# A Mamba block with a routed feed-forward: GpSimd's inflows of four units moved behind the scatters of their unit, and the scatters and lists laid out anew

## What is computed

```python
x = x + attn_ref(layernorm(x))        # attn_ref: below
x = x + ffn_ref(layernorm(x))         # top 2 of 8 experts, gated, width 344

# inside attn_ref, for each token l, channel d (256) and state n (16)
delta = softplus(dt @ dt_w.T + dt_b)
dA = exp(delta * A)                   # "decay"
dBu = delta * B * xc                  # "inflow"
h = dA * h + dBu                      # along the tokens: "scan", "state"
y = sum over n of h * C               # "product", summed on TensorE
y = (y + xc * D) * silu(z)            # then out_proj, and the feed-forward
```

## Time and profile before

| | |
|---|---|
| median of 3 runs | 848.82 us (848.8 to 850.25) |
| the profiled execution, its own time | 843.71 us |
| its span, first to last instruction | 841.0 us |
| VectorE busy | 739.6 us, 88% |
| TensorE busy (matmuls) | 649.6 us, 77% |
| GpSimd busy | 580.0 us, 69% |
| ScalarE busy | 506.9 us, 60% |
| mean granted clock of TensorE | 0.89 |

### The profile page before, as it was taken

The page is one execution under the profiler, slowest core; times in us unless marked ns, Lnnn a source line. Parts: engine busy times, 40 slices in busy tenths (PEclk is TensorE's granted clock), DMA queues, the critical chain, the costliest instruction groups (busy, mean ns, idle before and its releaser), DMA issues.

```text
span 841.0 us, 12622 instructions
## 1 busy us (share of the span) xinstructions
PE 649.6 (77%) x3545; PEld 465.1 (55%) x3545; DVE 739.6 (88%) x1147; ACT 506.9 (60%) x1091; POOL 580.0 (69%) x487
## 2 busy tenths in 40 slices
PE   4438688878778877787967877986876889898992
PEld 2124455545355536764657635863554556788992
DVE  1376998989999999999999999999999898686676
ACT  2545895876678577565856567464864775444441
POOL 1095675677977797688958897689855995456542
PEclk9659898989989898997889989897877899999996
DMA  6933233222323335543364336532423520123139
GB/s 177 269 97 101 91 111 111 83 88 90 115 75 101 104 105 182 160 134 114 114 192 135 107 101 189 154 124 97 132 86 104 179 85 24 45 55 93 54 102 272
DMA packets 80295, 99.92 MB, mean 119 GB/s; under 512 B 10263, under 2 KB 48099, under 8 KB 80211
## 3 DMA queue, kind: packets, MB, share of 16 engines
q1 hardware_dynamic: 75907, 90.21, 35.9%
q0 software_dynamic: 4320, 8.92, 3.0%
HBM read 87.56 MB, written 15.35 MB: 122 GB/s over the span
## 4 chain that ended last, share of the span: by engine, by line
DVE 36%; PE 33%; issue 18%; ACT 6%; POOL 4%; DMA 2%; SPq 1%; DVEq 1%; ACTq 0%; POOLq 0%
DVE state L1092 18%; PE work_front L1270 4%; DVE product L1102 4%; PE y L1310 4%; PE up L1432 2%; PE up L1421 2%; PE work_front L1276 2%; PE y L1306 2%; PE gate L1414 2%; POOL inflow L833 2%; DVE stats L1022 2%; ACT decay L956 1%; DVE silu_m L1235 1%; DVE arena L1067 1%; PE work_side L1354 1%
## 5 line engine op out<-in xcount | busy, mean ns | idle before, releaser
L833 POOL TENSOR_TENSOR inflow<-du,b_wide 128x1024 f32<-128x1024 f32 x128 | 315.5, 2468 | 145.1 <-DVE product L1102 92.1
L1092 DVE TENSOR_TENSOR_SCAN state<-decay,carry,inflow 128x512 f32<-128x512 f32 x192 | 234.8, 1264 | 6.5 <-ACT decay L956 6.5
L1102 DVE TENSOR_TENSOR product<-state,c_wide 128x1024 f32<-128x1024 f32 (+1 forms) x93 | 138.9, 1494 | 4.4 <-PE y L1306 3.3
L956 ACT ACTIVATE decay<-arena,a_neg 128x512 f32<-128x512 f32 x128 | 86.6, 688 | 60.6 <-DVE state L1092 56.8
L1306 PE MATMUL y<-ident,product 128*128 128x128 f32 x664 | 106.5, 305 | 20.5 <-DVE product L1102 20.5
L1306 PEld LDWEIGHTS y<-ident,product 128*128 128x128 f32 x664 | 87.4, 158 | 62.5 <-issue 34.7
L956 ACT ACTIVATE decay<-delta_odd,a_neg 128x512 f32<-128x512 f32 x128 | 86.5, 688 | 56.2 <-DVE state L1092 56.0
L863 POOL DMA_INDIRECT y_dram<-y_rows,x_rows x71 | 81.6, 1149 | 55.9 <-ACT y_rows L1012 49.2
L1310 PE MATMUL y<-h_rows,ident 128*128 128x512 f32 x180 | 100.9, 652 | 7.1 <-ACT h_rows L921 6.5
L857 POOL DMA_INDIRECT row_dram<-m_tok,place x64 | 74.2, 1159 | 24.4 <-issue 12.9
L1092 DVE TENSOR_TENSOR_SCAN state<-decay,inflow 128x512 f32<-128x512 f32 x64 | 74.5, 1203 | 6.1 <-ACT decay L956 3.6
(11 more groups left out here) (232 smaller groups left out, 1342.5 us busy)
## 6 DMA issues: line engine op xcount, KB each, us to landing
b_wide<-bc_dram SPq DMA_DIRECT2D x128, 256.0 KB, 3.3
c_wide<-bc_dram SPq DMA_DIRECT2D x93, 256.0 KB, 3.5
w_stage<-gate_up_dram SPq DMA_DIRECT2D x26, 344.0 KB, 4.4
x_rows<-row_dram SPq DMA_DIRECT2D x71, 65.0 KB, 2.1
arena<-gate_up_dram SPq DMA_DIRECT2D x8, 344.0 KB, 4.2
x_tok<-in_x SPq DMA_DIRECT2D x8, 256.0 KB, 5.8
out<-x_tok SPq DMA_DIRECT2D x7, 256.0 KB, 4.9
inflow<-y_dram SPq DMA_DIRECT2D x6, 256.0 KB, 4.5
```

The costliest lines, as they stand in the source:

```text
L833: e.tensor_tensor(inflow[:, key % 3], du[:, c % 2], b_wide[:, key % ROW_SLOTS:key % ROW_SLOTS + 1, :].to_broadcast([P, HALVES, CHUNK]), AL ...
L956: e.activation(decay_bank[h][:], delta[c % 2][:, h, :], ACT.Exp, scale=a_neg[:, h, n:n + 1]).then_inc(S["decay"], 1)
L1092: e.tensor_tensor_scan(state[:, key % STATE_SLOTS, h, :], decay_bank[h][:], inflow[:, key % 3, h, :], 0.0 if c % (SEQ // CHUNK) == 0 else ...
L1102: e.tensor_tensor(product[:, key % 2, :, :wide], state[:, key % STATE_SLOTS, :, :wide], c_wide[:, key % ROW_SLOTS:key % ROW_SLOTS + 1, :wi ...
```

## The change

In chunks 1 to 6, the inflows of the third to sixth unit (n = 2 to 5) are put at the end of unit i, behind the row of `SEND`, and no longer at its start; they wait for the product of the unit two before them and not three. For the unit n = 5 of these chunks the place of the inflow of i + 2 (n = 7) is behind the first parts of BACK and FRONT. `SEND` gives one scatter of the first slot to each of n = 0 to 3, `tag1` to n = 4, and two scatters of the second slot each to n = 5 and 6; `list1` goes to n = 7 and `list2` to n = 8 (they were in 6 and 7), and `list0` (it was in n = 2) is put at the end of unit n = 15, as soon as the places are known. The loads of a job's rows ask for the list and the last scatter, and the loads may come behind `send()` in the unit.

```diff
 SEND = [
-    ("tag0", ("scatter", 0, 0), ("scatter", 1, 0)),
-    (("scatter", 2, 0), ("scatter", 3, 0)),
-    ("list0",),
-    ("tag1", ("scatter", 0, 1), ("scatter", 1, 1)),
-    (),
+    ("tag0", ("scatter", 0, 0)),
+    (("scatter", 1, 0),),
+    (("scatter", 2, 0),),
+    (("scatter", 3, 0),),
+    ("tag1",),
+    (("scatter", 0, 1), ("scatter", 1, 1)),
     (("scatter", 2, 1), ("scatter", 3, 1)),
     ("list1",),
     ("list2",),
...
+LATE_INFLOW = (2, 6)
...
+def late_inflow(i):
+
+    return i < len(UNITS) and 0 < UNITS[i][0] < CHUNKS - 1 and LATE_INFLOW[0] <= UNITS[i][1] < LATE_INFLOW[1]
...
-            if (m < X_SLOTS or ("add", m - X_SLOTS) in done) and JOBS[m][0] in sent and ("load_x", m) not in done:
+            if (m < X_SLOTS or ("add", m - X_SLOTS) in done) and JOBS[m][0] in sent and JOBS[m][0] in listed and ("load_x", m) not in done:
...
+                if name == "scatter" and key[1:] == (SUB - 1, TOPK - 1):
+                    sent.add(key[0])
                 if name == "list2":
-                    sent.add(key)
                     listed.add(key)
...
+                if c in ROUNDS and c < CHUNKS - 3:
+                    put("list0", c)
...
-        fetch("inflow", i + 2)
+        if not late_inflow(i + 2) and not (0 < c < CHUNKS - 1 and n == LATE_INFLOW[1] - 1):
+            fetch("inflow", i + 2)
...
         put_all(back[0], front[0])
+        if ("inflow", i + 2) not in done and not late_inflow(i + 2):
+            fetch("inflow", i + 2)
         add()
...
-        any(load(q, i) for q in range(m, m + W_SLOTS))
-        send()
+        if any(load(q, i) for q in range(m, m + W_SLOTS)):
+            send()
+        else:
+            send()
+            any(load(q, i) for q in range(m, m + W_SLOTS))
...
         put("times_c", i)
+        if late_inflow(i + 2):
+            fetch("inflow", i + 2)
...
+                    behind = 2 if late_inflow(key) else 3
                     if key >= 3:
-                        if share[key - 3] < SUB:
-                            e.wait_ge(S["times_c"], products[key - 3])
+                        if share[key - behind] < SUB:
+                            e.wait_ge(S["times_c"], products[key - behind])
                         else:
-                            e.wait_ge(S["scan"], HALVES * (key - 2))
+                            e.wait_ge(S["scan"], HALVES * (key - behind + 1))
```

## The result

The kernel after the change takes 868.03 us (median of four runs, 862.52 to 868.29) against 848.90 for the kernel before beside it: a ratio of 1.0208 (1.0184 to 1.0231; the ratios here are estimated from the single runs and aren't quotients of two medians). In a later batch it was 863.5 against 850.89, 1.0172 (1.0117 to 1.0227). I had forecast 851.6, at most 861. The sign is right and the size is not.

A forecast was written before the change was run, and what follows sets the result against it. VectorE sets the pace, busy 739.6 of 841.0 us, stalled by GpSimd's inflows. The terms summed to +2.8 us, 843.71 to 846.5 in the profiled execution, 851.6 at the median; range 841 to 861.

The forecast's parts named there:

- n = 2, 4, 15: Chunks 1 to 6: product stalls shrink at n = 2 (-9.7 us) and n = 4 (-7.65); picking unstopped at n = 15 (-4.4).
- n = 5: Unit n = 5, chunks 1 to 6: two inflows back to back delay rstd2 and so the shift; +4.5 us.
- the new wait of the shift: At n = 5, VectorE idles before the shift until rstd2 is ready; 1.4 us six times.
- n = 6: Unit n = 6: gains in chunks 4 to 6, loses 0.5 in 2 and 3; -3.15 us.
- n = 8 and 9: Units n = 8 and 9: lists and x_sum keep GpSimd late; 5.9 and -1.0 us.
- The faster rival: The pair of scatters in n = 5 and 6 isn't held by a product, n = 7 costs nothing; 843.4 us, chance 0.30.
- n = 7: Unit n = 7, chunks 2 to 6: the inflow comes just ahead of the product, a new stall of 2.1; +8.2 us.
- five inflows whole: Upper bound of the n = 7 term, +11.8 us; its lower bound was nothing.
- n = 10 and 11: Units n = 10 and 11: GpSimd's backlog stops VectorE; +6.0 and +4.1 us.
- the pattern of unit 4.10: Chunk 4 before: three inflows in 9.03 us stopped L1067 at n = 10 for 1.96; taken for chunks 3, 5, 6.
- The slower rival: Late backlog: a second stop at n = 10 costs 2.2 us in chunks 3 to 6; 860.4 us, chance 0.20.
- the one that is late waits: A product and an inflow don't run side by side; the later one waits for the other's end.

The follow-up runs named there:

- e6: The kernel after with x_sum one unit later, in n = 8; 861.10 us, ratio 1.0121 to the kernel before.
- the first pair: First profiles of the kernels before and after, one each, unchanged; chunks 1 to 6 were 15.4 us longer in the kernel after.
- the second pair: Both kernels, before and after, profiled once more, unchanged; chunks 1 to 6 were 10.2 us longer in the kernel after.
- e2: The kernel after without late inflows: scatters spread, list0 in n = 15, list1 and list2 a unit later; 851.37 us, ratio 1.0009 to the kernel before.
- e5: e2 with the second slot's second pair of scatters in n = 8, lists in n = 9 and 10, jobs two units later; 831.02 us, ratio 0.9772.
- e8: e5 with tag1 in n = 5, the second slot's four scatters in n = 8 and 9, lists in n = 10 and 11; 821.15 us, ratio 0.9676.
- e3: The kernel after with the inflow of n = 6 instead of n = 7 behind the first parts, letting rstd2 in between; 863.04 us, ratio 1.0130.
- e7: e5 with the second slot's second pair of scatters back in n = 6, lists still in n = 9 and 10; 841.26 us, ratio 0.9916.

## Why the prediction was wrong

**Right.** That stalls of SBUF-only work by GpSimd's inflows are what can be moved; n = 2, 4, 15 within a microsecond, the first two partly by luck, since errors in single chunks cancel (at n = 4 I had -1.65, -1.7, -1.7 for chunks 4 to 6, and it was -0.1, -2.4, -2.4); n = 5 (+5.2 for +4.5), with the new wait of the shift, 6.4 us for 8.4, and with the shift (chunk 1) or xc (chunks 2 and 3) stopped behind it; list0 for nothing. n = 6 and n = 8 and 9 are off by one or two microseconds. The faster rival is refuted: scatters of the pair do get held, and n = 7 pays. Of the four scatters of units 3.5 and 3.6 in the kernel after two took 1.89 and 1.27 us instead of 0.96 (rows in the last section).

**Mis-sized: n = 7**, +14.6 for +8.2. I had one inflow at 2.1 us per chunk, less what it covers. Measured were 2.0, 3.2, 3.2, 3.3, 1.1 and 1.8. The missing piece in chunks 2 to 4 is `x_sum` behind the inflow, 1.22 each by e6; and chunk 1, for which I had nothing, pays too (0.84 of its 2.0 us is a wait for TensorE). It lies outside my +11.8 for "five inflows whole", since I took one inflow to be the worst that can happen to a product.

**Mis-sized: n = 10 and 11**, +4.1 for +10.1. I carried the pattern of unit 4.10 to three more chunks; it came in chunks 5 and 6 only, +2.4 each at n = 10. The slower rival, a second stop at n = 10, didn't happen. These two errors, +6.4 and -6.0 in the first pair, nearly cancel; it is luck that the sum over the units that I named is off by only 1.6 us (2.0 in the second pair).

**Missing: what the stalls had covered.** This is the step that failed. "Stall gone, time saved" was my rule at each unit, with nothing at n = 3 for what then arrives too early. It holds for the unit itself (n = 2 gave 9.5) and fails one or two units on: in chunks 3 to 6 VectorE came 1.4 to 2.4 us earlier to n = 3, and TensorE and ScalarE hadn't finished. The trace of before had such waits already, x_two once for 1.5 us and the scan for the decay 3.7 us; I had read them as small, not as a sign of how little slack lay behind the stalls. This is +6.7 (or 3.7) at n = 3 and +4.3 (or 1.7) in the other units without a term, 11.0 of the 12.6 us by which chunks 1 to 6 missed; in the second pair 5.4 of 7.4. That the waits come from VectorE's being early is read from the traces (e2 has 4.9 us before x_two without any late inflow); no run changed TensorE's or ScalarE's pace alone.

**What lies around.** My base was a profile 5.1 us shorter than its median, and I added that difference back as a constant, rightly. The remaining 2 to 4 us between the difference in chunks 1 to 6 and that of the medians (19.1 against 15.4, and 12.6 against 10.2) I can't place: the kernel after ran at 868.0 to 868.3 three times and at 862.5 once, with clocks of 0.871 to 0.875 and 0.882. That the time goes with the clock is seen; why the clock differs isn't.

**What stays open.** How much of e5 and e8 comes from the shares that the planner moved to ScalarE and TensorE, since the layout can't be changed without it in this kernel; how much TensorE's lower clock adds to the waits (e2 and e8 show that they come without one, at 0.91 and 0.92 against 0.90); and why the clock fell in e3.

## What to carry to other kernels

When VectorE and GpSimd keep each other off SBUF, price a move of GpSimd's work twice: the stalls it removes, and, one or two units later, the slack that the next engine (TensorE or ScalarE here) has left; of the VectorE time that was removed here, 1.4 of 20.0 us came back as idle time in e5, 12.6 of 42.9 in e8, and more than all of it in the change itself (with its new wait for rstd2). Keep two long GpSimd operations from running back to back ahead of anything VectorE waits for, and don't let a second SBUF operation follow one directly at a place where a wide VectorE instruction is due. Put the work that has slack (scatters, lists) where VectorE's units are long, and measure each half of a change alone: here the second pair of scatters in n = 8 was worth 10 us over n = 6 (e5 against e7, 10.9 of it in chunks 1 to 6), and the late inflows that came with the scatters in this change cost 5 to 17. e8 was 20 us faster than e7, but it also has `tag1`, the lists and the jobs a unit later and three products fewer on VectorE.

## What the hardware showed that I hadn't expected

- A VectorE product that had waited 2.1 us for an inflow was passed by `x_sum`, issued at 317.66 as the inflow ended (4.44 us long, 3.22 without it). The small operation `ahead` (L598), right behind the inflow in e6, took 1.20 us instead of 0.66 to 0.67 and let the product go first.
- Which of the two starts first by the profile doesn't decide. xc started at 304.55, the inflow at 304.57, and xc took 3.44 us; in unit 4.6 a half product was recorded 0.59 us before an inflow that directly followed a scatter, and took 3.51 us for 0.69. In the earlier trace rows it was the same with 468.51 and 468.61, so that "the one that is late waits" in the forecast isn't what those rows say. Behind another inflow it went the other way: the half product of 300.08 in 3.4 lost nothing, and the inflow beside it did (5.13 us for the block, 4.67 in 4.5). The Trainium skill, SBUF — State Buffer, section "Who interferes with whom", says that issue order decides who blocks; taken by the recorded starts, xc and the product of 4.6 would have gone through in their undisturbed time, and the traces don't bear that out. Whether a recorded start is the moment of issue, no run shows. Unit 4.6 of the kernel after:

```profile
408.59 3.51 DVE L1121 TENSOR_TENSOR product<-state,c_wide 128x512 f32<-128x512 f32 x1
```

```profile
408.19 0.97 POOL L876 DMA_INDIRECT row_dram<-m_tok,place  x1 [0.30 <-issue]
409.18 2.36 POOL L852 TENSOR_TENSOR inflow<-du,b_wide 128x1024 f32<-128x1024 f32 x1
```

- An indirect DMA that is started while a product or xc runs is held until shortly after its end, as the forecast had it. The one at 307.08 was started while xc ran (304.55 to 307.99) and ended at 308.97, 0.98 us behind it; the one at 312.80 was started in the half product of 311.00 to 313.19 and ended 0.88 us behind it; the one at 309.28 ran beside scans, in 0.96. The inference of the Trainium skill, SBUF — State Buffer, section "Who interferes with whom", that tensor_tensor leaves descriptor writing alone does not hold here. GpSimd in the kernel after, units 3.5 and 3.6:

```profile
307.08 1.89 POOL L876 DMA_INDIRECT row_dram<-m_tok,place  x1 [0.18 <-issue]
309.28 0.96 POOL L876 DMA_INDIRECT row_dram<-m_tok,place  x1 [0.30 <-issue]
310.27 2.36 POOL L852 TENSOR_TENSOR inflow<-du,b_wide 128x1024 f32<-128x1024 f32 x1
312.80 1.27 POOL L876 DMA_INDIRECT row_dram<-m_tok,place  x1 [0.17 <-issue]
```

- The stretch behind chunk 6 took 202.3 us in one profile of the kernel before and 209.9 in another, same code. At one place in it the second has TensorE standing 3.59 us for y_rows, and the first has no idle time there.
